# Stacked score matmuls in an attention stage, and a bf16 output projection in a linear attention stage

## What is computed

```
L0: x1 = ln(x) * (scale1 + 1) + shift1
    q, k, v = x1 @ qkv_w.T + bias          # 16 heads of 16 channels
    q = l2norm(q) * exp(scale_mul);  k = l2norm(k)
    o = softmax(q @ k.T) @ v
    x = x + (o @ proj_w.T + proj_b) * gamma1
    x = x + ffn(ln(x) * (scale2 + 1) + shift2) * gamma2      # 1024 wide, gelu
L1: q, k, v = layer_norm(x) @ Wq, Wk, Wv (+ biases)
    q = softmax(q over channels);  k = softmax(k over tokens)
    y = q @ (k.T @ v)
    h = silu(layer_norm(y) * (1 + scale) + shift) @ out_W + out_b
    x = x + cond * h
```

## Time and profile before

| | |
|---|---|
| median of 3 runs | 1221.93 us (1221.79 to 1222.16) |
| profiled execution | 1226.43 us, of which its span is 1224.7 us |
| mean granted TensorE clock | 0.973 |
| busy share TensorE, VectorE, ScalarE, GpSimd | 91%, 75%, 66%, 71% |
| setup, attention | 0 to 24, 24 to 466 us |
| feed-forward stage | 466 to about 840 us |
| linear stage | about 840 to 1224.7 us |

### The profile page before, as it was taken

The page is one execution under the profiler, slowest core; times in us unless marked ns, Lnnn a source line. Parts: engine busy times, 40 slices in busy tenths (PEclk is TensorE's granted clock), DMA queues, the critical chain, the costliest instruction groups (busy, mean ns, idle before and its releaser), DMA issues. The chain is left out here.

```text
span 1224.7 us, 37712 instructions
## 1 busy us (share of the span) xinstructions
PE 1111.7 (91%) x11946; PEld 820.0 (67%) x12098; DVE 912.5 (75%) x2274; ACT 813.0 (66%) x2205; POOL 870.7 (71%) x1147
## 2 busy tenths in 40 slices
PE   4688999999999864999999999996999999999996
PEld 3476787878778762666667666664666666766664
DVE  6678888888888727465554645625999999999985
ACT  2687899999999732535454444542777777777774
POOL 4688899999999744457666576642577777777777
PEclk9899999999999976999999999998999999999999
DMA  7563333333333322100101001010011111111112
GB/s 262 165 145 56 65 66 66 65 67 65 68 62 70 62 45 61 35 19 18 34 17 34 17 17 35 18 35 1 15 43 42 39 60 39 41 57 39 43 56 83
DMA packets 138945, 68.13 MB, mean 56 GB/s; under 512 B 76544, under 2 KB 137600, under 8 KB 138880
## 3 DMA queue, kind: packets, MB, share of 16 engines
q1 hardware_dynamic: 110480, 41.32, 15.2%
q10 hardware_dynamic: 28400, 25.99, 7.2%
HBM read 41.58 MB, written 8.65 MB: 41 GB/s over the span
## 5 line engine op out<-in xcount | busy, mean ns | idle before, releaser
L1139 PE MATMUL f_ps_y<-w_fc,f_h_split 128*128 128x256 bf16 x1536 | 172.8, 273 | 1.4 <-DVE f_branch L1258 1.4
L1166 PE MATMUL f_ps_h<-f_x_split,w_fc 128*128 128x512 bf16 x737 | 166.5, 383 | 4.3 <-DVE f_biases L1289 1.4
L667 POOL TENSOR_TENSOR e_split<-e_full,e_split 128x1024 bf16<-128x1024 f32 x64 | 136.5, 2133 | 42.7 <-ACT e_full L747 42.4
L1139 PEld LDWEIGHTS f_ps_y<-w_fc,f_h_split 128*128 128x128 bf16 x1536 | 150.2, 98 | 22.5 <-issue 1.7
L1500 ACT ACTIVATE l_z_t<-l_ps_yt,shift,scale 128x64 f32<-128x64 f32 x256 | 82.6, 403 | 92.6 <-PE l_ps_yt L1566 57.1
L1266 DVE TENSOR_TENSOR f_h_split<-f_h,f_h_split 128x512 bf16<-128x512 f32 x64 | 64.0, 1002 | 104.3 <-ACT f_h L1125 104.3
L1166 PEld LDWEIGHTS f_ps_h<-f_x_split,w_fc 128*128 128x128 bf16 x768 | 75.6, 99 | 88.8 <-issue 3.4
L1124 ACT ACTIVATE f_h_split<-f_ps_h,columns 128x512 bf16<-128x512 f32 x128 | 89.1, 696 | 66.6 <-POOL f_h_split L1085 36.2
L807 PE MATMUL ps_s<-qk_t,k_pairs 128*128 128x64 bf16 x3072 | 103.4, 195 | 24.3 <-DMA k_pairs<-qk_t 23.1
L807 PEld LDWEIGHTS ps_s<-qk_t,k_pairs 128*128 128x128 bf16 x3072 | 98.6, 99 | 34.3 <-DMA k_pairs<-qk_t 18.5
L1085 POOL TENSOR_TENSOR f_h_split<-f_h,f_h_split 128x512 bf16<-128x512 f32 x64 | 79.7, 1256 | 36.7 <-ACT f_h L1125 36.7
(11 more groups left out here) (183 smaller groups left out, 3129.2 us busy)
## 6 DMA issues: line engine op xcount, KB each, us to landing
v_pairs<-v_split SPq DMA_DIRECT2D x128, 66.0 KB, 2.1
k_pairs<-qk_t SPq DMA_DIRECT2D x256, 32.0 KB, 2.3
gain<-gammas SPq DMA_DIRECT2D x64, 128.0 KB, 3.1
f_gain<-gammas ACTq DMA_DIRECT2D x32, 256.0 KB, 4.4
l_gate<-in_cond ACTq DMA_DIRECT2D x128, 64.0 KB, 2.5
out<-x_all ACTq DMA_DIRECT2D x16, 512.0 KB, 2.9
x_all<-in_x SPq DMA_DIRECT2D x13, 512.0 KB, 6.0
fc_full<-in_L_cond_fc_w SPq DMA_DIRECT2D x2, 1024.0 KB, 8.4
```

The costliest lines, as they stand in the source:

```text
L667: pool.tensor_tensor(flat(e_split[a][:, LO]), flat(e_full[:]), flat(e_split[a][:, HI]), ALU.subtract).then_inc(e_lo_made, 1)
L1139: last = pe.matmul(ps_y[:, i], h_split[a][:, hs, f, i * P:(i + 1) * P], m.w_fc2[:, ws, f], start=(f == 0 and k == 0), stop=(f == F_CHUNKS ...
L1166: last = pe.matmul(ps_h[f % 4][:], m.w_fc1[:, ws, c, f * P:(f + 1) * P], x2_split[a][:, xs, c], start=(k == 0 and c == 0), stop=(k == 2 an ...
```

## The change

Setup: scale1 is made with its sign turned, since x_hat now comes with its sign turned; k_stack (4096 words a partition) is cleared in place of k_pairs (8192); q and k weights are laid out so that the four groups of a chunk lie next to each other. Semaphores are merged.

Attention: the three splits are stacked along the contraction, 96 rows, so that one matmul does what three did; SyncE fills k_stack and q_stack with nine DMAs for two tiles. VectorE does both halves of the modulation. One two-element product on GpSimd takes the place of two one-element products. The squares are written head by head. The norms are summed into the bank of ps_qk, and qkv waits for norms_weighted in place of qk_biased. All lists are in another order.

Linear stage: w_out in two bf16 parts, three passes; silu is split by a copy on ScalarE and a subtraction on GpSimd; x_hat moves from VectorE to ScalarE; the first channel half of y is modulated on VectorE; project, residual, add and store are one, one, two and four steps later.

```diff
@@ stack of k and q, attention (in place of place_k)
+            def stack_qk(t):
...
+                sp.wait_ge(qk_lo_made, t.n + 1)
+                two = slice(t.u - 1, t.u + 1)
+                for j, (k, q) in enumerate(SPLITS):
+                    for r in range(2):
+                        rows = slice((2 * j + r) * HD, (2 * j + r + 1) * HD)
+                        sp.dma_start(k_stack[rows, t.u // 2, :, :, :, :, r].rearrange("p g t c s k -> p (g t c s) k"),
+                                     qk_t[r * L:(r + 1) * L, 1, k, two].rearrange("p t c (s k) -> p (t c s) k", s=SEQ)
+                                     ).then_inc(qk_stacked[t.u // 2], 16)
+                    rows = slice(2 * j * HD, 2 * (j + 1) * HD)
+                    sp.dma_start(q_stack[rows, t.u // 2].rearrange("p g t c k -> p (g t c k)"),
+                                 qk_t[:, 0, q, two].rearrange("p t c k -> p (t c k)")).then_inc(qk_stacked[t.u // 2], 16)
...
-            pipeline(sp, [(6, place_v), (6, place_k), (0, load_later), (9, load_gain)])
+            pipeline(sp, [(0, load_later), (6, stack_qk), (9, load_gain), (6, place_v)])
@@ GpSimd, attention
-                pool.tensor_tensor(heads(qk_hat[a][:]), heads(qk[a][:]), over_channels(factors[a][:]), ALU.mult
+                pool.tensor_tensor(strided(qk_hat[a][:]), strided(qk[a][:]), over_strided(factors[a][:]), ALU.mult
...
-            pipeline(pool, [(12, add), (0, split_fc), (0, rstd_of), (2, x1_low), (8, e_lo), (4, normalise)])
+            pipeline(pool, [(12, add), (0, rstd_of), (0, split_fc), (2, x1_low), (4, normalise), (8, e_lo)])
@@ ScalarE, attention
-                act.activation(squares[:], qk[a][:], ACT.Square).then_inc(squared, 1)
+                act.activation(head_of(squares[:]).rearrange("p x g e -> p x e g"), strided(qk[a][:]), ACT.Square).then_inc(squared, 1)
...
-            pipeline(act, [(2, modulate_second), (4, v_hi), (4, square), (2, x1_high), (8, high_exponentials),
-                           (10, o_hi), (4, logs), (5, qk_hi), (8, full_exponentials), (4, factor), (0, split_fc),
-                           (0, hat)])
+            pipeline(act, [(4, square), (5, qk_hi), (4, v_hi), (8, high_exponentials), (10, o_hi), (2, x1_high),
+                           (4, logs), (4, factor), (8, full_exponentials), (0, split_fc), (0, hat)])
@@ TensorE, attention
-                            for i, (k, q) in enumerate(SPLITS):
-                                last = pe.matmul(ps_s[:, s, G_ * c + g],
-                                                 k_pairs[:, t.slot(4), k, c, s, g].rearrange("p r k -> p (r k)"),
-                                                 qk_t[:, 0, t.slot(4), q, c, s * L:(s + 1) * L], start=(i == 0), stop=(i == 2))
+                            last = pe.matmul(ps_s[:, s, G_ * c + g], k_stack[0:DEEP, t.slot(4) // 2, g, t.u % 2, c, s].rearrange("p r k -> p (r k)"),
+                                             q_stack[0:DEEP, t.slot(4) // 2, g, t.u % 2, c, own], start=True, stop=True)
...
-                reuse(pe, qk_biased, t, 1)
+                reuse(pe, norms_weighted, t, 1)
@@ VectorE, attention
-                dve.tensor_reduce(norms[a][:], heads(squares[:]), X_AXIS, ALU.add).then_inc(norms_made, 1)
+                dve.tensor_reduce(ps_norms, by_head(squares[:]),
+                                  X_AXIS, ALU.add).then_inc(norms_made, 1)
...
-            pipeline(dve, [(2, modulate), (4, biases), (10, outputs), (-1, statistics), (4, v_low), (0, aggregate),
-                           (4, reduce_norms), (10, o_low), (5, qk_lo), (11, residual)])
+            pipeline(dve, [(10, outputs), (4, biases), (-1, statistics), (0, aggregate), (2, modulate), (5, qk_lo),
+                           (4, v_low), (4, reduce_norms), (10, o_low), (11, residual)])
@@ feed-forward stage, once
+                    act.activation(m.w_out3[:, HI], out3_full[:], ACT.Copy).then_inc(out3_hi_made, 1)
+                    dve.tensor_tensor(m.w_out3[:, LO], out3_full[:], m.w_out3[:, HI], ALU.subtract)
@@ linear stage
-            pipeline(pool, [(5, softmax), (10, silus), (8, last_inverse_deviations), (-1, inverse_deviations),
-                            (12, add)])
+            pipeline(pool, [(14, add), (11, silu_low), (10, silus), (8, last_inverse_deviations),
+                            (-1, inverse_deviations), (4, softmax)])
...
+            def hat(t):
...
+                act.activation(x_hat[a][:, None, 1:], t.rows(m.x_all)[:, :, 1:], ACT.Identity, bias=minus_rstd[a][:, 1:2],
+                               scale=minus_rstd[a][:, 0:1]).then_inc(x_hat_made, 1)
...
+                act.activation(silu_split[a][:, HI], silu[a][:], ACT.Copy).then_inc(silu_hi_made, 1)
...
-            pipeline(act, [(3, v_high), (9, load_gate), (9, modulate), (1, x3_high), (3, k_exponentials),
-                           (3, q_exponentials), (5, k_high), (5, q_copy), (9, tanhs), (13, store)])
+            pipeline(act, [(9, load_gate), (1, x3_high), (17, store), (5, k_high), (3, k_exponentials),
+                           (9, modulate_second), (5, q_copy), (2, v_high), (-1, hat), (3, q_exponentials),
+                           (10, silu_high), (9, tanhs)])
...
-                for c in range(NC_):
-                    last = pe.matmul(ps_out[:], silu[a][:, c], m.w_out3[:, c], start=False, stop=(c == NC_ - 1))
+                for i, (zs, ws) in enumerate(SPLITS):
+                    for c in range(NC_):
+                        last = pe.matmul(ps_out[:], silu_split[a][:, zs, c], m.w_out3[:, ws, c],
+                                         start=False, stop=(i == 2 and c == NC_ - 1))
```

310 lines of the change are left out of this document (168 added, 142 removed).

## The result

The changed kernel takes 1217.94 us (median of 7 runs, 1215.45 to 1221.78), beside 1222.16 us for the kernel before (median of 7, 1221.37 to 1226.38). The ratio is 0.9958, with a 95% interval of 0.9942 to 0.9975. I had forecast 1196 us and a range of 1184 to 1212: it is faster, as said, but by a sixth of the size. The profiled executions differ by as much: 1221.78 us with a span of 1220.0, against 1226.43 and 1224.7.

A forecast was written before the change was run, and what follows sets the result against it. Bounds: in attention a loop through SyncE's queue (12.04 us for two tiles), in the linear stage TensorE (5.64 us). Terms -7.8 - 7 - 1 - 12 + 2 = -25.8 us; set against the 1221.93 us median: 1196 us, range 1184 to 1212.

The forecast's parts named there:

- The new wait: Attention: qk matmuls wait for norms_weighted instead of qk_biased, with 0.5 us to spare after latencies, so no added time.
- Setup: Start of the kernel: half of the 6.88 us memset goes, taken as -1 us (0 to -3.4).
- The squares: Attention, ScalarE: writing the squares at a 64-byte step still takes 632 ns, as before.
- rival 2: Attention: the squares cost twice as much (1.26 us), giving 6.1 us a tile and 1206 us; chance 0.10.
- my VectorE sum: Attention: two further modulations at 0.26 us each raise VectorE from 5.34 to 5.86 us a tile, making it the bound.
- rival 3: Attention: the nine DMAs land late, each k DMA having 512 pieces instead of 256; 1204 to 1212 us, chance 0.08.
- End of attention: Last attention tiles: turning q and k ahead of the scores and shorter scores save 7 us (3 to 10).
- The linear stage: Linear stage: 5.64 becomes 5.45 us a tile, -0.20 us over 60 tiles, so -12 us (-15 to 0).
- Rival 1: Linear stage gains nothing: a chain across engines, most likely ScalarE with its gate DMAs, becomes the bound; 1208 us, chance 0.13.
- the drain: End of the linear stage: one step deeper, a copy and a subtraction more, a shorter projection; +2 us (0 to +4).
- rival 5: Attention: the granted clock falls with TensorE at 83% busy, making the program 100 us longer; chance 0.03.

The follow-up runs named there:

- n1: The changed kernel with the norms summed into SBUF again and the qk matmuls waiting for qk_biased; 1212.04 us, ratio 0.9897 to the kernel before.
- b1: The kernel before with only the norms summed in PSUM and the qk matmuls waiting for the weighted norms; 1223.04 us, ratio 0.9987.
- p1: n1 with TensorE computing the scores ahead of the turning of q and k; 1234.28 us, ratio 1.0078 to the kernel before.
- g1: n1 with the linear stage's gate DMAs and stores issued by SyncE; 1215.16 us, ratio 0.9925 to the kernel before.
- n4: The changed kernel with TensorE's linear-stage list in its earlier order, the projection at its new depth; 1219.10 us, ratio 0.9943 to the kernel before.
- c7: n1 with squares kept as bf16, written side by side and read by VectorE at an 8-byte step; 1203.08 us, ratio 0.9825 to the kernel before.
- c4: n1 with, in the linear stage, two modulations back on ScalarE and gate DMAs and stores on SyncE; 1209.78 us, ratio 0.9884 to the kernel before.
- n2: The changed kernel with squares written side by side and VectorE's sum reading at a 16-byte step; 1223.27 us, ratio 0.9983 to the kernel before.
- c1: n1 with ScalarE reading qk at a 16-byte step and writing squares head by head, side by side; 1217.66 us, ratio 0.9944 to the kernel before.
- c6: n1 with squares written and summed side by side, which computes other norms; 1203.26 us, ratio 0.9804 to the kernel before.
- s1: n1 with v_pairs ahead of the stacked scores' DMAs in SyncE's queue; 1300.38 us, ratio 1.0602 to the kernel before.

## Why the prediction missed

**The new wait (norms in PSUM), predicted 0, measured +10 us in the profiles and 7.5 by the ratios: the step that failed.** I wrote that VectorE does "o_low, residual and outputs (1.9 us) before it wants them: 0.5 us to spare". The steady state bears this out: there TensorE's weight load waits for the norms 0.7 us in 20 tiles. But these three stages work on tiles six and seven behind the one whose norms are made. In the first ten steps they do not run, the cover is gone, and with it the spare time; the ring of 7.10 us replaced a tile of 4.5. I had asked for the cover of every edit in the steady state and not for the fill, and had taken the matmuls at 1.2 us, which is their time at the higher clock. n1 shows the size (first e_split 71.12 to 60.91, ratio 0.9958 to 0.9897), b1 that it takes PSUM and the new orders together; which of the new orders stays open.

**Setup, predicted -1, measured nothing.** The memset is 3.4 us shorter, and the first turning of x comes no earlier: the term's end at 0 was right.

**The squares, predicted 632 ns, measured 1084: a mis-sized term, and rival 2's mechanism.** I gave it 0.10. Its consequence is smaller than the rival's 0.2 us a tile, 0.15 (5.949 against 5.795), and it did not bring 6.1 us, because the rest of my VectorE sum was too high: with squares of 632 ns a tile takes 5.79 us, not 5.90. VectorE's busy time rose by 0.25 us a tile (5.34 to 5.59, 113.61 us by 20.3 tiles), not by 0.52: the two further modulations add 0.47 (1.07 in a row against 0.60), and back to back the instructions overlap by some 0.08 us each, which busy times added up do not show. The two errors partly cancel, and that is luck. The gain of a steady tile was 0.085 us where I had 0.156: the base was 6.035, not 6.056, and the end 5.950, not 5.90. Over the 50 tiles of my sum that is -4.3 us; the -5.8 between the first and the 58th tile holds something of the fill as well.

**TensorE's scores and the DMAs.** 16 matmuls took 0.64 us, not 0.5; TensorE was no longer the bound, so it cost nothing that shows. The nine DMAs (rival 3) landed in 4.0 us (k_stack) and 4.5 (q_stack), where k_pairs took 2.3. I had named a landing over 4 us as a sign of being wrong; the steady state had room for it, and the scores waited for them 0.3 us in 20 steady tiles. At the end a wait of 4 us was still there once, against my forecast:

```profile
443.81 1.04 PE L802 MATMUL ps_s<-q_stack,k_stack 96*128 96x64 bf16 x16 [4.18 <-DMA q_stack<-qk_t]
```

**End of attention, predicted -7, measured -6.3.** Right in size; of the reason, the place of turn_qk in TensorE's list, p1 bears out 1 to 3 us at most. That the sum fits is luck as far as the runs show.

**The linear stage, predicted -12, measured -4.5: a mis-sized term.** Mechanism and bound were right: TensorE stopped being the bound, and VectorE became it. The base, 5.64 us, was right inside the loop (5.647). But VectorE takes 5.56 us there, not 5.41, and I had taken 5.45: I had added busy times, and the queue also has 0.23 us before l_kq and about 0.3 us at every fourth tile, where the loop starts over. Each tile so gained 0.09 us, not 0.20. The "0.16 us idle" of TensorE in the earlier trace rows was no idle time: five records of the qkv matmuls stand there where six ran. The first 56 steps gave -7.3 (315.54 to 308.23), and the last seven took 2.8 back (24.27 to 27.07): they ran at 3.5 us before and now at 3.9, with the new copy and subtraction as the likely reason. I had costed the drain at +2 for what follows the last tile alone, and there it came out at +1.9. Rival 1, that the stage gains nothing because ScalarE and its gate DMAs become the bound, did not come: g1 took the DMAs out of ScalarE's queue and the pace stayed.

**The clock, rival 5.** In steady attention it was 1.00, as forecast. It fell where I had not looked, in the fill: 0.63, with waits of 2.66 us before the slow matmuls (though not behind every such wait, as n4 shows). The Trainium skill, TensorE: Matmul & The Clock Gate (Part 1), ties the lower clock to idleness, which agrees; the rival's price of 100 us was for the wrong place.

## What to carry to other kernels

A wait that is covered by later stages of a software pipeline is uncovered while the pipeline fills and drains: cost each new wait a second time with the stages of old tiles taken out, and at the lower clock (here 0.63) if TensorE then waits between its groups. Before taking an operation's time over to another layout, look at the step in bytes of what is read and what is written; a smaller type took the price away here (c7). And a busy share of 100% does not name the bound: TensorE showed 176.00 of 176 us in the changed linear stage, n4 took 0.26 us a tile out of its transpositions and the pace stayed, while c4 took two modulations from VectorE and the pace moved. Before two busy times are compared, count the records of each group: missing ones look like idle time.

## What the runs showed of the hardware

- 512 f32 elements per partition on ScalarE: 629 to 632 ns side by side, 1084 written at a 64-byte step, 1136 read at a 16-byte step. The sum on VectorE: 676 to 684 ns side by side, 1091 at 16 bytes, 674 at 8 bytes in bf16 (n2, c1, c6, c7 and the changed kernel).
- Summing into PSUM instead of SBUF cost VectorE nothing that shows: 684 against 676 ns, and the weighting that follows got shorter, 191 instead of 244 (the changed kernel against n1).
- DMAs between SBUF tiles in 128-byte pieces landed in 4.0 to 4.5 us at a share of the DMA engines' time of 0.86, and the scores waited for them 0.3 us in 20 steady tiles.
- Another order of SyncE's list (s1 against n1) cost 1.0602 / 0.9897, so 7%, with no instruction added.
